# A recommendation tower on one core: three buffers for gathered rows, GpSimd's gathers without a wait for gram matrices, and the weights' preparation placed among the first two tiles' steps

## The reference

```python
e = stack([tbl_f[ids[:, f]] for f in range(26)], axis=1)      # 2048 x 26 x 64
x = layer_norm(dense @ Wd.T, gd, bd)                           # 2048 x 128
y = layer_norm(einsum('bnd,ed->bne', e, Ws), gs, bs)           # 26 rows of 128 a sample
y = layer_norm(einsum('bne,pn->bep', y, Wsi), gsi, bsi)        # mixed to 32 rows
T = concatenate([x[:, None, :], swapaxes(y, 1, 2)], axis=1)    # 33 rows of 128
Z = einsum('bnd,bmd->bnm', T, T)                               # gram matrix of a sample
out = layer_norm(Z[:, tril] @ Wl.T, gl, bl) * mask             # 528 -> 512, first 384 kept
h = relu(concatenate([out, dense], 1) @ W_top1 + b_top1)
h = relu(h @ W_top2 + b_top2)
return h @ W_top3                                              # 2048 x 1
```

## Time and profile before

| | |
|---|---|
| median of 3 runs | 608.56 us (607.56 to 610.67) |
| profiled execution | 609.85 us, its span 608.0 us |
| busy: TensorE, its weight loads | 523.0 (86%), 389.3 (64%) |
| busy: VectorE | 499.1 (82%) |
| busy: GpSimd | 401.0 (66%) |
| busy: ScalarE | 338.4 (56%) |
| chain that ended last, by engine | PE 40%, POOL 25%, issue 14%, DVE 10%, DMA 5%, ACT 5% |
| mean granted clock of TensorE | 0.989 |

### The profile page before, as it was taken

The page is one execution under the profiler, slowest core; times in us unless marked ns, Lnnn a source line. Parts: engine busy times, 40 slices in busy tenths (PEclk is TensorE's granted clock), DMA queues, the critical chain, the costliest instruction groups (busy, mean ns, idle before and its releaser), DMA issues.

```text
span 608.0 us, 17689 instructions
## 1 busy us (share of the span) xinstructions
PE 523.0 (86%) x6955; PEld 389.3 (64%) x6955; DVE 499.1 (82%) x977; ACT 338.4 (56%) x922; POOL 401.0 (66%) x422
## 2 busy tenths in 40 slices
PE   2466858999998989999999989898998999998996
PEld 1354636585867667675758576667667585857575
DVE  5985599998889796888889898979888898988750
ACT  4003364666566565656566666657574666666642
POOL 6777456777777777777777777777777777760000
PEclk9999997999999998999999999999999999999999
DMA  7311011111111111111111111111111111110000
GB/s 171 109 25 38 17 26 24 36 28 28 38 28 36 28 38 27 36 26 37 27 36 30 27 37 28 37 28 37 27 37 28 37 28 27 29 28 3 1 3 1
DMA packets 22611, 20.23 MB, mean 33 GB/s; under 512 B 12016, under 2 KB 14720, under 8 KB 22528
## 3 DMA queue, kind: packets, MB, share of 16 engines
q0 software_dynamic: 13312, 13.66, 11.7%
q1 hardware_dynamic: 8400, 4.33, 2.7%
q10 hardware_dynamic: 816, 1.11, 0.6%
HBM read 19.07 MB, written 0.01 MB: 31 GB/s over the span
## 4 chain that ended last, share of the span: by engine, by line
PE 40%; POOL 25%; issue 14%; DVE 10%; DMA 5%; ACT 5%; SPq 0%; POOLq 0%; ACTq 0%; DVEq 0%
POOL emb L239 25%; PE b_l L381 7%; PE b_y L326 6%; PE b_mix L314 6%; DMA emb<-in_tbl,idx 4%; PE b_a L305 4%; PE b_z L338 4%; PE b_l L407 3%; PE b_a L296 2%; PE b_l L399 2%; ACT nrm L518 1%; DVE V L869 1%; ACT embt L505 1%; PE b_l L369 1%; PE b_l L414 1%
## 5 line engine op out<-in xcount | busy, mean ns | idle before, releaser
L239 POOL DMA_INDIRECT emb<-in_tbl,idx x416 | 400.3, 962 | 143.7 <-issue 122.3
L851 DVE TENSOR_TENSOR yb<-b_y,bias_y 128x1024 f32<-128x1024 f32 x64 | 78.3, 1223 | 38.7 <-PE b_y L326 36.8
L505 ACT ACTIVATE embt<-b_a 128x512 f32<-128x512 f32 (+1 forms) x64 | 32.7, 512 | 125.9 <-PE b_a L296 125.9
L869 DVE TENSOR_TENSOR V<-yb,rstd_y 128x256 f32<-128x256 f32 x256 | 91.9, 421 | 2.2
L326 PE MATMUL b_y<-mixed,projw 64*128 64x512 f32 x256 | 73.5, 650 | 13.9 <-ACT mixed L524 13.5
L858 DVE TENSOR_REDUCE var_y<-sq 128x32 f32<-128x1024 f32 x64 | 77.1, 1205 | 2.4 <-ACT sq L529 2.4
L305 PE MATMUL b_a<-gram_w,embt 128*128 128x128 f32 x416 | 65.3, 299 | 15.1 <-ACT embt L505 15.1
L314 PEld LDWEIGHTS b_mix<-mix,byn 128*128 128x128 f32 x512 | 65.5, 200 | 16.1 <-issue 13.4
L305 PEld LDWEIGHTS b_a<-gram_w,embt 128*128 128x128 f32 x416 | 56.7, 205 | 29.2 <-ACT embt L505 19.6
L314 PE MATMUL b_mix<-mix,byn 128*128 128x128 f32 x512 | 73.3, 288 | 1.9 <-DVE byn L846 1.7
L524 ACT ACTIVATE mixed<-b_mix 128x512 f32<-128x512 f32 x64 | 38.3, 598 | 58.6 <-PE b_mix L314 58.1
(11 more groups left out here) (134 smaller groups left out, 722.0 us busy)
## 6 DMA issues: line engine op xcount, KB each, us to landing
emb<-in_tbl,idx POOLq DMA_INDIRECT x416, 2.4
dense<-in_r_dense_t SPq DMA_DIRECT2D x16, 128.0 KB, 2.2
V<-in_L_rec_Wl ACTq DMA_DIRECT2D x1, 1056.0 KB, 5.3
w<-in_W_top SPq DMA_DIRECT2D x2, 512.0 KB
w<-in_W_top SPq DMA_DIRECT2D x1, 768.0 KB
out_y<-y_sb SPq DMA_DIRECT2D x16, 0.5 KB
idx<-in_ids SPq DMA_DIRECT2D x1, 195.0 KB, 5.1
wd<-in_L_rec_Wd SPq DMA_DIRECT2D x1, 128.0 KB
```

The lines of the kernel that those rows point to most:

```text
L239: pool.indirect_dma_start(out=emb[t % 2][:, f, :], out_offset=None, in_=tables[f], in_offset=bass.IndirectOffsetOnAxis(ap=idx[:, t, f:f + ...
L851: nc.vector.tensor_tensor(yb[c % 2][:, :, :, :].rearrange("e h s p -> e (h s) p"), b_y[:, :, :].rearrange("e h (s p) -> e (h s) p", p=NP), ...
L869: last = nc.vector.tensor_tensor(V[t % 2][:, j2, c, m:m + 2, :, 0:NP].rearrange("e m q p -> e (m q) p"), yb[c % 2][:, j2, 4 * m:4 * m + 8, :],
```

## The change

`emb` has three buffers instead of two (`NE = 3`), and all that indexes them goes by `t % NE`. GpSimd's wait for `gram_done` and the list `GATE` are gone; its waits for `nrm_ready` and `act_nrm` look at tile t - 3.

The preparation is moved. On VectorE `fold(0)` goes behind the first norms of round 0, `fold(1)` behind the second, `prepare_mlp` and `fold_sums` behind the third and the first `normalize`, `prepare_gain` to the end of round 0; the five `prepare_wlt` go into round 1, after `add_bias` of chunk 1, after the second norms, after `add_bias` of chunk 2, and around `add_bias` of chunk 3 and `scale` of chunk 2. On TensorE `prepare_b1` goes behind the norms of batch 2, `prepare_gain` behind tile 0's dense product, and the five `prepare_wlt` between round 1's steps. The diff's block of TensorE from `layer3(t3)` to `norms(t0, 2)` only shows as moved; its order is kept.

```diff
--- before.py
+++ after.py
@@ -40,7 +40,7 @@
 
 
 
-GATE = (1, 3, 4, 4)
+NE = 3
 
 
 def tri(i, j):
@@ -91,7 +91,7 @@
         wmean = sb("wmean", [P, RC]); b1p = sb("b1p", [P, 4])
 
         idx = sb("idx", [P, T, NF], INT32)
-        emb = [sb(f"emb{h}", [P, NF, D]) for h in range(2)]
+        emb = [sb(f"emb{h}", [P, NF, D]) for h in range(NE)]
         nrm = sb("nrm", [P, D, NP])
         byn = [sb(f"byn{h}", [P, NJ, D]) for h in range(2)]
         embt = sb("embt", [P, 4, P]); prod = [sb(f"prod{h}", [P, 8, D]) for h in range(2)]
@@ -136,7 +136,7 @@
             sem("wsq_zero"), sem("wsq_act"), sem("wsq_ready"), sem("gain_ready"), sem("wlt_ready"))
         idx_loaded = [sem(f"idx_loaded{h}") for h in range(2)]
 
-        gathered = [[sem(f"gathered{h}{b}") for b in range(4)] for h in range(2)]
+        gathered = [[sem(f"gathered{h}{b}") for b in range(4)] for h in range(NE)]
         emb_transposed, embt_copied, gw_done = sem("emb_transposed"), sem("embt_copied"), sem("gw_done")
         prod_done, varn_done, varm_done, stdn_done, rstdn_done, nrm_ready, act_nrm, byn_ready = (
             sem("prod_done"), sem("varn_done"), sem("varm_done"), sem("stdn_done"), sem("rstdn_done"), sem("nrm_ready"), sem("act_nrm"), sem("byn_ready"))
@@ -230,15 +230,14 @@
                 if t < 2:
                     pool.wait_ge(idx_loaded[t], 16)
                 for b in range(4):
-                    after(pool, nrm_ready, 2 * (t - 2) + b // 2 + 1)
+                    after(pool, nrm_ready, 2 * (t - NE) + b // 2 + 1)
                     if b == 0:
-                        after(pool, act_nrm, ACT_PIECES * (t - 1))
-
-                    after(pool, gram_done, 4 * (t - 2) + GATE[b])
+                        after(pool, act_nrm, ACT_PIECES * (t - NE + 1))
+
                     for f in features(b):
-                        pool.indirect_dma_start(out=emb[t % 2][:, f, :], out_offset=None, in_=tables[f],
+                        pool.indirect_dma_start(out=emb[t % NE][:, f, :], out_offset=None, in_=tables[f],
                                                 in_offset=bass.IndirectOffsetOnAxis(ap=idx[:, t, f:f + 1], axis=0)
-                                                ).then_inc(gathered[t % 2][b], 16)
+                                                ).then_inc(gathered[t % NE][b], 16)
 
         @block.tensor
         def _(pe):
@@ -290,10 +289,10 @@
                 last.then_inc(wlt_mm, 1)
 
             def transposes(t, b):
-                pe.wait_ge(gathered[t % 2][b], 16 * len(features(b)) * (t // 2 + 1))
+                pe.wait_ge(gathered[t % NE][b], 16 * len(features(b)) * (t // NE + 1))
                 after(pe, prod_done, 4 * t + b)
                 for n, c in enumerate(BATCHES[b]):
-                    last = nc.tensor.transpose(b_a[:, n * P:(n + 1) * P], emb[t % 2][:, 2 * c:2 * c + 2, :].rearrange("p n d -> p (n d)"),
+                    last = nc.tensor.transpose(b_a[:, n * P:(n + 1) * P], emb[t % NE][:, 2 * c:2 * c + 2, :].rearrange("p n d -> p (n d)"),
                                                ident[:, :])
                 last.then_inc(emb_transposed, 1)
 
@@ -427,6 +426,8 @@
                 if real(t1):
                     project(t1, 0)
                     mix_features(t1, 1)
+                if u == 1:
+                    prepare_wlt(0)
                 if real(t3):
                     layer2(t3)
                 if real(t0):
@@ -434,36 +435,38 @@
                 if real(t1):
                     mix_features(t1, 2)
                     project(t1, 1)
+                if u == 1:
+                    prepare_wlt(1)
                 if real(t2):
                     pair_rows(t2)
                 if real(t0):
                     norms(t0, 1)
+                if u == 1:
+                    prepare_wlt(2)
+                if real(t3):
+                    layer3(t3)
+                if real(t1):
+                    dense_back(t1)
+                if real(t2):
+                    x_rows(t2)
+                if real(t1):
+                    project(t1, 2)
+                if real(t2):
+                    interact(t2)
+                if real(t0):
+                    transposes(t0, 2)
+                if real(t1):
+                    gram(t1, 0)
+                if u == 1:
+                    prepare_wlt(3)
+                if real(t2):
+                    interact_x(t2)
+                if real(t0):
+                    norms(t0, 2)
                 if u == 0:
                     prepare_b1()
-                    prepare_gain()
-                    prepare_wlt(0)
-                    prepare_wlt(1)
-                    prepare_wlt(2)
-                    prepare_wlt(3)
+                if u == 1:
                     prepare_wlt(4)
-                if real(t3):
-                    layer3(t3)
-                if real(t1):
-                    dense_back(t1)
-                if real(t2):
-                    x_rows(t2)
-                if real(t1):
-                    project(t1, 2)
-                if real(t2):
-                    interact(t2)
-                if real(t0):
-                    transposes(t0, 2)
-                if real(t1):
-                    gram(t1, 0)
-                if real(t2):
-                    interact_x(t2)
-                if real(t0):
-                    norms(t0, 2)
                 if real(t1):
                     mix_features(t1, 3)
                     project(t1, 3)
@@ -482,6 +485,8 @@
                     gram(t1, 2)
                 if real(t0):
                     dense_project(t0)
+                if u == 0:
+                    prepare_gain()
                 if real(t2):
                     layer1(t2, 1)
 
@@ -515,7 +520,7 @@
                 act.wait_ge(rstdn_done, 2 * t + 1)
                 after(act, byn_ready, 2 * t)
                 for f in range(lo, hi):
-                    last = nc.scalar.activation(nrm[:, :, f], emb[t % 2][:, f, :], ACT.Copy, scale=rstd_n[:, f:f + 1])
+                    last = nc.scalar.activation(nrm[:, :, f], emb[t % NE][:, f, :], ACT.Copy, scale=rstd_n[:, f:f + 1])
                 last.then_inc(act_nrm, 1)
 
             def copy_mixed(t, c):
@@ -810,7 +815,7 @@
                 dve.wait_ge(gw_done, 4 * t + b + 1)
                 after(dve, varn_done, 4 * t + b - 1)
                 nc.vector.tensor_tensor(prod[b % 2][:, 0:n, :], b_a[:, 0:n * D].rearrange("p (n d) -> p n d", d=D),
-                                        emb[t % 2][:, f0:f0 + n, :], ALU.mult).then_inc(prod_done, 1)
+                                        emb[t % NE][:, f0:f0 + n, :], ALU.mult).then_inc(prod_done, 1)
                 dve.wait_ge(prod_done, 4 * t + b + 1)
                 after(dve, varm_done, 2 * (t - 1) + b // 2 + 1)
                 nc.vector.tensor_reduce(var_n[:, f0:f0 + n], prod[b % 2][:, 0:n, :], AXX, ALU.add).then_inc(varn_done, 1)
@@ -832,7 +837,7 @@
                 dve.wait_ge(rstdn_done, 2 * t + k + 1)
                 after(dve, byn_ready, 2 * t)
                 for f in range(max(f0, ACT_FEATURES), f0 + n, 2):
-                    last = nc.vector.tensor_tensor(nrm[:, :, f:f + 2].rearrange("p d n -> p n d"), emb[t % 2][:, f:f + 2, :],
+                    last = nc.vector.tensor_tensor(nrm[:, :, f:f + 2].rearrange("p d n -> p n d"), emb[t % NE][:, f:f + 2, :],
                                                    rstd_n[:, f:f + 2].unsqueeze(2).broadcast_to([P, 2, D]), ALU.mult)
                 last.then_inc(nrm_ready, 1)
 
@@ -894,15 +899,12 @@
 
             prepare()
             prepare_wsq()
-            fold(0)
             for u in range(T + 2):
                 t0, t1, t2 = u, u - 1, u - 2
                 if real(t0):
                     norms(t0, 0)
                 if u == 0:
-                    fold(1)
-                    prepare_mlp()
-                    fold_sums()
+                    fold(0)
                 if real(t1):
                     add_bias(t1, 0)
                 if real(t2):
@@ -910,17 +912,19 @@
                 if real(t1):
                     variance(t1, 0)
                     add_bias(t1, 1)
+                if u == 1:
+                    prepare_wlt(0)
                 if real(t0):
                     norms(t0, 1)
                 if u == 0:
-                    prepare_gain()
-                    prepare_wlt(0)
+                    fold(1)
+                if u == 1:
                     prepare_wlt(1)
-                    prepare_wlt(2)
-                    prepare_wlt(3)
                 if real(t1):
                     scale(t1, 0)
                     add_bias(t1, 2)
+                if u == 1:
+                    prepare_wlt(2)
                 if real(t0):
                     bound_n(t0, 0)
                 if real(t1):
@@ -931,12 +935,17 @@
                     norms(t0, 2)
                     normalize(t0, 0)
                 if u == 0:
-                    prepare_wlt(4)
+                    prepare_mlp()
+                    fold_sums()
```

(16 more changed lines are left out.)

## The result

The changed kernel takes 600.17 us (597.54 to 600.48), the kernel before 608.06 beside it: a ratio of 0.9846, 95% interval 0.9813 to 0.9879. The profiled execution took 600.01 us with a span of 598.0, against 609.85 and 608.0. The forecast was 602, with 596 to 609.5.

A forecast was written before the change was run, and what follows sets the result against it. GpSimd's gathers, 32.66 us a tile, were taken to bound, with TensorE needing 32.4. Gather waits removed (-8.5) and preparation spread (+1.0) sum to -7.5 us, forecasting 602 us, range 596 to 609.5.

The forecast's parts named there:

- What bounds: Whole kernel: GpSimd's gathers, 32.66 us a tile, are the fullest; TensorE runs in step, ahead by a hair.
- TensorE's own pace: Tiles 3 to 15: without its waits for gathers TensorE needs 32.4 us a tile instead of 33.03.
- the bound of 11: Upper bound on the 8.5 us gain from TensorE's gather waits, if shorter tiles let the clock stand better.
- The check at 32.41: TensorE's first transposes from 459.23 to 491.64, no wait at the end: one tile of 32.41 us supporting 32.4.
- GpSimd: Gathers: 32.66 us a tile, giving back 0.3 a tile; last gather at 524.8, some lead left at tile 15.
- The floor by GpSimd: Whole kernel: if TensorE could follow the gathers, all would end 19.6 us earlier, at 590 us; chance 0.02.
- Tile 0: First tile: VectorE's share ends at 55.5, first mix at 57.8 instead of 65.79, 8.0 us won.
- Tile 1's round: VectorE there: five moved prepare_wlt add 8.2 us on the path; transposes to byn end at 98.7 against 97.7.
- Part 2: Spreading the preparation over tiles 0 and 1 hands back what it won: net +1.0 us, bounds -2.5 and +4.
- D: Slower rival: TensorE thin in tile 1, clock low through it and tile 2's first 20 us, 614 us; chance 0.08.
- B: Rival: spreading gains, as tile 1 uses 3.3 us of idle and the clock is high from first mix; 597, chance 0.17.
- Tail: From tile 15's first transpose to the end: unchanged at 83.8 us.

The follow-up runs named there:

- Part 1 alone: Kernel before with three buffers and GpSimd's wait for gram matrices removed, the weights' preparation left where it was: 600.26 us, ratio 0.985.
- the pair without the mean: Changed kernel with the mean left out of the five prepare_wlt, 599.82 us; the same with one gather fewer from tile 3 on, 594.48 us.
- the two-buffer kernel: Changed kernel with two buffers instead of three, still without GpSimd's wait for gram matrices: 599.74 us, ratio 0.9833.

## Why the prediction was right, point by point

**What bounds.** Right: GpSimd paced the kernel, TensorE was in step with it by a hair, and what the change could give was TensorE's waits for gathers. Part 1 alone gives the whole result.

**TensorE's own pace.** 32.4 a tile was forecast; 32.28 was measured. The 0.1 is the fall of the clock at 229.8 us in the profile before (1.2 us over 12 tiles), which stood in the rate; it followed a transpose that had waited 1.55 us for a gather. Over 12 tiles 9.0 us were gained against 8.0 forecast; a better clock had been counted as a possible gain, in the bound of 11. The check at 32.41 was a single tile; with tiles of 32.1 and 32.4 to 32.6 in turn, one of them can't tell 32.4 from 32.28. And what was called TensorE's own need is a ring with ScalarE in it: with a wait of TensorE shortened the pace stayed.

**GpSimd.** Here a step was mis-sized, and the answer was right by luck: 2.0 us of lead in the changed kernel's profile, 0.8 and none in two others. The last gather was forecast for 524.8 and came at 531.27. The rate was taken as (400.3 + 122.3) / 16 = 32.66, but 122.3 us of "issue" stood in 400 places and there are 416 gathers. In the others the waits' own figures hold the space of 0.3 each, 4.5 us in all, and it stays when the wait goes: now 125.9 us in 413 places. With 1.7 us more busy and a first gather 0.5 later that is the 6.5 us missed. With 402.0 busy that is 33.0 a tile. So GpSimd gives back 0.6 to 0.7 us a tile, not 0.3 (the lead went from 11.1 to 3.6 in 12 tiles), and little was left at tile 15; the pair without the mean shows what comes then. The floor by GpSimd is an estimate of 510.8 (512.82 less 2.0) + 83.8 for a tail without a fall + 1.9 around the span = 596.5 us, not 590; the kernel with `fold(0)` first, its first gather 0.6 us earlier, took 596.57 and 595.43 at the least.

**Tile 0.** First mix forecast at 57.8, measured 55.98; VectorE's share ends at 53.97, not 55.5. The 3 us of small waits were 1.7 too many: from 22.48 to 53.97 are 31.5 us, 30.2 of them busy. The idle of 5.4 us in front of the first norms came as forecast (5.63).

**Tile 1's round.** Forecast 27.0 + 8.2 + 0.7 = 35.9 us from the first `yb`, measured 35.5, with the moved steps on the path in full. `byn` at 98.7 forecast, 96.3 measured, 2.0 of the 2.4 from tile 0. Net of Part 2: +1.0 forecast, -1.4 against the profile before. But Part 1 alone has `byn` at 96.15 too, with the preparation unmoved. The profile before was late there by its own clock: tile 1's first projection took 2.08 us at 68.64, with Part 1 alone 1.13 at 68.80. The net worth of Part 2 beside Part 1 is zero within the 2 us of such differences (600.17 and 600.26).

**The clock and D.** TensorE was thin in tile 1's round and the granted clock fell twice, low for 17 us instead of 10.2, as D's mechanism says. (When the round began both kernels were still at the lower level, by the durations: before until some 72 us, after until some 63.) The Trainium skill's rule (TensorE: Matmul & The Clock Gate, What's actually happening) has activity release the clock; the trace agrees in direction: TensorE was busy 5.10 of 6.8 us ahead of the fall at 70.5 and 6.58 of 10.2 ahead of that at 87.6, against 25.40 of 27.0 from 98 to 125, where the clock stayed high. D's price of 12 us didn't come: VectorE held the end of that round, and by 97.8 the clock was high again. The run with matmuls in the idle places had 6.8 us less of low clock and was no earlier at tile 3. B's condition, a high clock from the first mix, was not met here (the mix at 55.98 and the projection behind it ran at the lower level); in the two-buffer kernel it nearly was, and brought 2.1 us at `byn` and 0.8 at tile 3.

**Tail.** Not unchanged: 85.2 against 83.8, the fall at 548.4.

The sum by term, against the span: -9.0 (forecast -8.0 between tiles 3 and 15), -2.4 up to tile 3 (forecast +0.5: -0.5 for waits, +1.0), +1.4 in the tail (forecast 0). Total -10.0 against -7.5. Of the 10.0, the fall at 229.8 and the late rise of the clock in the profile before (1.6 at `byn` of tile 1) are 2.8 us, and the tail's fall took 1.4: some 8.6 us are the change's own, an estimate.

## What to carry to other kernels

When a wait goes that keeps one engine late, look for the pace of the engine that it feeds (from a stretch that has no wait at its end) and for the lead that remains at the last tile: small errors in a rate, here 0.3 us a tile, decide over sixteen tiles which engine bounds. Count the instructions against the places of an idle figure before taking a rate from it. Two gains that work through the same wait don't add: each was worth something alone, and the second nothing beside the first; and steps moved from an idle engine's early list into a full round only change where they are paid. Here `fold(0)` left where the engine is idle anyway gives a slightly better kernel than the changed one, 596.57 us, some 2 us of which are its own. And before a difference of 1 or 2 us is given a cause, look whether two kernels with the same instructions differ by as much.

## What the runs showed of the hardware

A wait of TensorE for a transfer cost more than the idle time that the profile shows for it: 0.55 us for a shown 0.39 (at 326.62 before). Removing the 6.4 us shown between tiles 3 and 15 gave 9.0, of which 1.2 were a fall of the clock.

The granted clock fell to 0.50 for 3.4 us some 2 us after single stands of TensorE of 1.55 us (before, at 227.53) and 1.67 us (after, at 546.75), which cost 1.2 and 1.4 us. In the 15.4 us ahead of the falls TensorE was busy 11.90 and 11.87. The stand of 1.6 to 1.7 us ahead of the last tile's mix is in all thirteen profiles, and in six of them the fall follows it; in the others, the kernel before among them (558.28), it doesn't. What decides it was not found.

A gather of 128 rows takes GpSimd 0.944 us in the median and a space of 0.30 us; in the mean of the changed kernel's 416 it is 0.966, and the longest are 1.6 to 1.9 us, in tile 0's round. From tile 2 on that makes 1.266 us a gather, 32.9 a tile.
